# Weighing a chunk of keys in two halves of the queries, with two maxima tiles in front of each half

## What is computed

```python
scores = jnp.einsum('bhqd,bhkd->bhqk', Q, K) / math.sqrt(Dh)
scores = jnp.where(causal, scores, jnp.finfo(scores.dtype).min)
attn = jax.nn.softmax(scores, axis=-1)
y = jnp.einsum('bhqk,bhkd->bhqd', attn, V)
```

## Time and profile before

| | us |
|---|---|
| median of three runs | 5375.74 |
| lowest, highest | 5335.63, 5381.57 |
| the profiled execution | 5351.09 |
| its span, first to last instruction | 5349.2 |
| sparse attention, within it | about 266 to 967 |
| dense attentions, within it | about 1394 to 4597 |

### The profile page before, as it was taken

How to read it: one execution, slowest core, us unless ns; L and a number is a source line. 1 busy time by engine, 2 the same in 40 slices (tenths; PEclk the granted TensorE clock), 3 DMA queues, 4 the chain that set the end, 5 groups by cost and what they waited for, 6 DMA issues and landing times.

```text
span 5349.2 us, 82616 instructions
## 1 busy us (share of the span) xinstructions
PE 4794.5 (90%) x31872; PEld 2551.8 (48%) x31872; DVE 4064.9 (76%) x9211; ACT 2852.4 (53%) x3317; POOL 284.4 (5%) x339
## 2 busy tenths in 40 slices
PE   5377989676599999999999999999999999899999
PEld 4244445566244333443334443333443333588888
DVE  7465757577488898889998888998889977455555
ACT  3234545322155666666676666677566777432322
POOL 2010000133000000000000000000000000300000
PEclk8778989887578999999999999999999999899999
DMA  4633221355600030030120210200300000201010
GB/s 151 172 72 66 43 53 27 111 189 192 125 17 13 7 52 12 21 54 9 15 38 15 40 32 9 37 16 23 59 10 5 9 9 10 69 21 40 21 40 9
DMA packets 226730, 255.84 MB, mean 48 GB/s; under 512 B 69329, under 2 KB 170705, under 8 KB 224017
## 3 DMA queue, kind: packets, MB, share of 16 engines
q1 hardware_dynamic: 216512, 190.12, 12.5%
q0 software_dynamic: 9824, 60.43, 7.0%
HBM read 143.99 MB, written 104.92 MB: 47 GB/s over the span
## 4 chain that ended last, share of the span: by engine, by line
PE 70%; DVE 19%; issue 5%; DMA 4%; ACT 2%; SPq 1%; POOL 0%; DVEq 0%; ACTq 0%; POOLq 0%
PE psum L782 22%; PE psum L713 19%; PE psum L76 13%; DVE maxes_dense L862 11%; PE psum L741 4%; PE psum L679 3%; PE psum L702 2%; DMA queries_sparse<-neg_rows_sparse 1%; PE psum L723 1%; PE psum L750 1%; PE psum L1541 1%; DVE masked_scores_dense L855 1%; DMA x_in<-in_L_attn_hidden_states 1%; DMA keys_sparse<-parts_scratch 1%; PE psum L709 1%
## 5 line engine op out<-in xcount | busy, mean ns | idle before, releaser
L819 ACT ACTIVATE probs_dense<-psum 128x1024 f32<-128x1024 f32 (+3 forms) x2304 | 2068.4, 950 | 996.7 <-PE psum L741 746.7
L862 DVE TENSOR_REDUCE maxes_dense<-psum 128x1 f32<-128x512 f32 x3584 | 2227.8, 683 | 227.3 <-PE psum L713 226.2
L713 PE MATMUL psum<-keys_dense,queries_dense 48*128 48x512 f32 (+3 forms) x4608 | 1553.6, 477 | 138.1 <-DMA queries_dense<-parts_scratch 54.8
L713 PEld LDWEIGHTS psum<-keys_dense,queries_dense 48*128 48x128 f32 x4608 | 667.5, 191 | 1490.8 <-DVE maxes_dense L862 1142.1
L782 PE MATMUL psum<-probs_dense,values_dense 128*32 128x512 f32 (+3 forms) x9216 | 1176.6, 588 | 0.0
L741 PE MATMUL psum<-queries_dense,keys_dense 50*128 50x512 f32 (+3 forms) x4608 | 809.3, 407 | 11.8 <-ACT probs_dense L819 11.5
L855 DVE CUSTOM_DVE_ANT_0 masked_scores_dense<-psum,causal_add 128x128 f32<-128x128 f32 (+3 forms) x1024 | 452.2, 488 | 175.6 <-PE psum L713 156.0
L741 PEld LDWEIGHTS psum<-queries_dense,keys_dense 50*128 50x128 f32 x4608 | 448.6, 193 | 106.8 <-ACT probs_dense L819 60.8
L855 DVE CUSTOM_DVE_ANT_0 masked_scores_sparse<-psum,after_add 128x512 f32<-128x512 f32 x512 | 326.4, 688 | 173.2 <-PE psum L702 172.2
L1648 ACT ACTIVATE activated<-psum 128x512 f32<-128x512 f32 x208 | 124.7, 599 | 414.1 <-PE psum L76 401.6
L819 ACT ACTIVATE probs_sparse<-psum 128x1024 f32<-128x1024 f32 x224 | 217.6, 1022 | 207.3 <-PE psum L679 78.9
(11 more groups left out here) (297 smaller groups left out, 5379.9 us busy)
## 6 DMA issues: line engine op xcount, KB each, us to landing
v_scratch<-ve_s SPq DMA_DIRECT2D x96, 256.0 KB, 2.7
parts_scratch<-part_high SPq DMA_DIRECT2D x24, 1024.0 KB, 4.2
parts_scratch<-part_low SPq DMA_DIRECT2D x24, 1024.0 KB, 6.7
queries_dense<-parts_scratch SPq DMA_DIRECT2D x384, 64.0 KB
keys_dense<-parts_scratch POOLq DMA_DIRECT2D x42, 512.0 KB, 17.7
values_dense<-v_scratch POOLq DMA_DIRECT2D x8, 2048.0 KB, 34.5
queries_sparse<-parts_scratch SPq DMA_DIRECT2D x192, 64.0 KB
keys_sparse<-parts_scratch POOLq DMA_DIRECT2D x18, 512.0 KB, 17.6
```

The costliest lines, as they stand in the source:

```text
L713: m = pe.matmul(bank[:, 0:width], q[rows(h, TROWS), h // 2, b * P:(b + 1) * P], k[rows(h, TROWS), h // 2, kc * STRIP:kc * STRIP + width], ...
L819: act.activation(probs[i % 6][:, :, first_col:STRIP], psum[:, at2:at2 + 2, first_col:STRIP], ACT.Exp, scale=SCALE, **extra).then_inc(exp_d ...
L862: m = dve.tensor_reduce(mx[:, h * BLOCKS + b, kc:kc + 1], bank, AX.X, ALU.max)
```

## The change

The order within a chunk's iteration becomes: four scores, then twice two tiles and half of the weighing of chunk c-1. The first half of the weighing is queries 0 to 255, the second 256 to 511. On the diagonal a half that has no query left is skipped: the third and fourth diagonal chunks have only a second half. Chunk 0 of a unit is weighed whole, in the place of its second half. In the sparse kernel's own-block chunk the halves are two blocks each. The semaphore that says that a chunk is weighed is raised by the second half. "Out" stands right behind the scores of chunk 1.

```diff
             for c in range(sizes[n]):
                 m = ends[n] - sizes[n] + c
-                emit_tiles(4 * (m + lead(n)) + 2)
                 for h in range(GROUP):
                     order.append(("score", n, (m, c, h)))
-                    if n >= 1 and c == 1 and h == 3:
-                        order.append(("out", n - 1, None))
-                    if h % 2 == 1:
-                        emit_tiles(4 * (m + lead(n)) + (2, 4)[h // 2])
-                if c >= 1:
-                    order.append(("weigh", n, (m - 1, c - 1)))
-            order.append(("weigh", n, (m, c)))
+                if n >= 1 and c == 1:
+                    order.append(("out", n - 1, None))
+                for half in range(2):
+                    emit_tiles(4 * (m + lead(n)) + 2 * half + 2)
+                    if c >= 1:
+                        order.append(("weigh", n, (m - 1, c - 1, half)))
+            order.append(("weigh", n, (m, c, 0)))
+            order.append(("weigh", n, (m, c, 1)))
...
-                        m_at, c = what
-                        if c == 0:
+                        m_at, c, half = what
+                        if c == 0 and half == 1:
                             pe.wait_ge(values_in[n // STRIPS % 2], 16 * (n // STRIPS // 2 + 1))
...
                         pe.wait_ge(exp_done, 2 * m_at + 2)
                         local = sparse and c == NSTR // P
-                        for b in (range(BLOCKS) if local else (None,)):
+                        first_col = max(half * STRIP // 2 if c else 0, 0 if sparse else (c - BLOCKS * j) * P)
+                        last_col = (half + 1) * STRIP // 2 if c else half * STRIP
+                        if first_col >= last_col:
+                            continue
+                        for b in (range(first_col // P, last_col // P) if local else (None,)):
...
-                                    cols, vt = slice(max(0, c - BLOCKS * j) * P, STRIP), v[:, c, own_rows]
+                                    cols, vt = slice(first_col, last_col), v[:, c, own_rows]
...
-                        m.then_inc(weighed, 1)
+                        if half == 1:
+                            m.then_inc(weighed, 1)
```

More of the change, by code:

```diff
@@ L778, in attend_pe @@
                                 elif sparse:
-                                    cols, vt = slice(0, STRIP), str_values[n // STRIPS % 2][:, c, own_rows]
+                                    cols, vt = slice(first_col, last_col), str_values[n // STRIPS % 2][:, c, own_rows]
                                 else:
-                                    cols, vt = slice(max(0, c - BLOCKS * j) * P, STRIP), v[:, c, own_rows]
+                                    cols, vt = slice(first_col, last_col), v[:, c, own_rows]
                                 m = pe.matmul(psum[own_rows, 4, cols], vt, probs[(2 * m_at + h // 2) % 6][:, h % 2, cols],
```

## The result

The changed kernel takes 5968.62 us (median of four runs, 5890.93 to 5968.85) against 5364.26 for the kernel before (four runs, 5335.63 to 5381.57). The ratio is 1.110, with a 95% interval of 1.099 to 1.120. The forecast was slower, 5590 us with a range up to 5730: the sign was right, the size was not.

A forecast was written before the change was run, and what follows sets the result against it. It took a loop between TensorE and VectorE, neither full, to bound the kernel. Terms 35 + 110 + 11 + 26 + 13 + 35 = 230 us on 5351 or 5376 gave 5581 or 5606, stated as 5590 us, range 5440 to 5730.

The forecast's parts named there:

- 35 + 110 + 11 + 26: Dense-stage costs in us: plain chunks +35, starts and diagonals of 56 units +110, strip 0's units +11, narrow tiles +26.
- Plain chunk: Dense chunk off the diagonal at full clock: period 2.75 us for 2.70, +0.045 each over 784 chunks.
- T1 to T4: In a plain chunk, from the first tile's start to the fourth's, which waits for the first's bank: 1.18 us.
- iterations on the diagonal: Diagonal chunks: scores and masks no longer hidden, less what the weighing saves; +0.38, +0.21, +0.35 and +0.41 us, in turn.
- the 2.9 to 3.1 named as a sign: Sign that the forecast is right: iterations on the diagonal near 2.9 to 3.1 us.
- the unit starts: Chunks 0 and 1 of a dense unit: unhidden scores +0.47 us and earlier "out" +0.15, so 0.62 a unit.
- Low clock: Dense chunks at clock 0.5: 4.37 us for 4.16, some 76 chunks, +13 us beyond what is counted.
- The clock falls more often: Rival, at unit starts where TensorE waits for VectorE: twice as much time at 0.5, 5770 us; chance 0.09.
- The sparse term: Sparse stage: 32 units, four iterations each with a second turn, 0.24 to 0.30 us each; +35 us, bounds nothing and +60.
- The clock making up for the loss: Rival: TensorE waits less, so dense clock stays full and the sparse stage gains too; about 5400 us, chance 0.07.
- VectorE as the bound: Rival: turns cost nothing, so a plain chunk takes VectorE's own 2.40 us; 235 us less, 5120 us, chance 0.06.
- Back-to-back issue gap: Skill rule: products at full clock are N/2.4 + 2.5 ns apart; read as making halves and turns free, but not taken.

The follow-up runs named there:

- e4: The kernel before, with chunks 0 and 1 of every unit in the changed order (four scores, then four tiles), weighings whole; 5585.18 us.
- e3: The changed kernel, with chunks 0 and 1 of every unit in the order of the kernel before, weighing whole there; 5636.18 us.
- e5: The changed kernel, with the score products of chunk 1 of every dense unit issued three times; 5755.07 us.
- e1: The kernel before in its old order, each weighing done as two halves one right behind the other; 5341.33 us in one execution.
- e2: The changed kernel with the weighing whole, in the place of its second half; 6404.5 us.
- e9: Against the kernel before: same sparse stage and chunks 0 and 1; other dense chunks put the second tile pair between the scores, weighing in halves; 5489.37 us, ratio 1.026.
- e11: The changed kernel with the third tile of a dense chunk issued twice, full-width tiles only; 5892.61 us.
- e6: The kernel before with the score products of chunks 0 and 1 of every dense unit issued twice; 5354 us, ratio 1.000.
- e13: e9 with the score products of chunks 0 and 1 of every dense unit issued three times; 5370 us, ratio 1.004 to the kernel before.
- e14: e9 with the score products of chunks 0 and 1 of every dense unit issued twice; 5361 us, ratio 0.999 to the kernel before.

## Why the prediction was wrong

- **The order at full clock: right.** Forecast for the dense stage 35 + 110 + 11 + 26 = 182 us; measured 163. Plain chunk 2.75 forecast and measured. T1 to T4 was forecast at 1.18: T4 starts 0.43 before the second half at 3003.80, which is 1.18 behind T1 at 3002.19. The first three iterations on the diagonal take 2.91, 3.01 and 2.72 (means at full clock, scores to scores) for 2.66, 2.71 and 2.33 before. They grew by 0.25, 0.31 and 0.39 where 0.38, 0.21 and 0.35 were forecast, the same in sum; the third lies below the 2.9 to 3.1 named as a sign. By e4 the unit starts cost 36 us, which was forecast as 56 x 0.62 = 35; by e3 the chunks cost 137, forecast 147.
- **The step that failed is "Low clock": "Some 76 chunks are at this clock: +13 beyond what is counted."** It carried the low-clock time of the kernel before, 315 us, into the changed one as if it were a given of the stage. It was 1158 us, and the term came to 312 us (estimated as above) and not 13.
- **The rival was at the right place at the wrong price.** "The clock falls more often" pointed to the place named just above it, the start of a unit, "where TensorE waits for VectorE tile after tile; that stretch loses four scores". e4 and e5 show that place to be the cause of most of the falls. I doubled the time at the low clock. It rose by a factor of 3.7, since I had counted falls and not their length: the periods begun in the stage went from 30 of 8.5 us to 51 of 22 us, and the long ones come only with the changed chunks (e3, e4). The chance of 0.09 was too low: an order that thins TensorE's work exactly where the clock already falls should have had a much larger one.
- **The sparse term was too small.** 35 us forecast, bounds 0 to 60; measured 94 from the order and 42 from the clock. Of the 94, 27 are the unit starts (e4), which the sum left out for the sparse stage though it had them for the dense one; the chunks are 64 (e3).
- **The clock making up for the loss** was argued from TensorE waiting less in a plain chunk. That is so (0.27 for 0.46 us) and helped nothing: of the periods that begin in the stage only one begins in a plain chunk, before as after.
- **VectorE as the bound: no.** VectorE idles 0.27 a chunk after, 0.22 before. A turn between tiles and weighing costs what the rows said. "TensorEngine Tiling (Array Packing)" of the Trainium skill, section "Key Properties", says that a change of tiling mode drains the engine. The trace fits this: 0.33 from a tile pair to a half, where the columns of the pair need 0.23. The other rule that the prediction took from the Trainium skill, the distance in "Back-to-back issue gap", is given there for isolated products; that it holds whatever they are, so that turns are free, was read into it, and the plain chunk of 2.75 and not 2.40 decides against it.

Not settled: which property of the chunk holds the clock down. It is not the width of the products (e1), and it does not take two turns (e2). Thin work over the whole chunk fits e2, but at full clock it does not fit e9, whose chunk does the same products in 2.50 us and had 13 long periods, and e11 was too weak to show it. One thing goes with the long periods in every run: where a chunk at the low clock takes 4.16 us (before, e1, e4, e6), none that began in the stage was over 25 us, and where it takes 4.32 or more, there are 2 to 24 of them. No run here changes that time alone, so it is a trace to follow and not a cause. The period carried in at the start of the dense stage, 119.5 us long before, says besides that the old order can stay low too.

## What to carry to other kernels

Before you price a new order, look at where the granted clock falls, and ask whether the new order leaves TensorE thinner at just those places; the low-clock time of the kernel before is no constant. Price a fall by how long it lasts under the new order too. If a stretch must wait, repeated products with the same result can hold the clock. Here they paid where much time was spent at the low clock (e5), and broke even where little was (e6, e13, e14).

## What was unexpected of the hardware

- The clock stayed at 0.50 for up to 99 us while TensorE ran chunk behind chunk, busy 99% of them by the profile (3220.7 to 3319.7). In the order of before every fall within the dense stage was over within 20.5 us, but the period carried in lasted 119.5.
- The start added 280 us of low-clock time alone, the chunks 173, and both together 843 (724 in a second profile of the same dense code).
- 64 x 8 added products of up to 512 columns made the changed kernel 3.6% faster.
- The first pair of products behind a weighing, whichever it is, takes 0.34 us and the next 0.23. The trace has the first pair's weight load starting only with the pair itself (both at 2703.95 in the trace of before).
